# The head of a decoder layer's last stage: order of the second tile's scores, fill matmuls, and VectorE's order

## What is computed

```python
x = x + matmul(fake_quant(layernorm(x)), fake_quant(ctx))      # "x_product"
h = layernorm(x)
q = h @ Wq_w.T                    # router, 16 columns
scores = q @ keys.T               # 64 experts
gate = softmax over the 16 largest of each row, 0 elsewhere
z = (h @ A_w.T)                   # 512 columns, 8 for each expert, times gate
x = x + z_gated @ B_w.T * 2       # "out_product"
```

## Time and profile before

| | |
|---|---|
| time, median of 3 runs | 1102.18 us (1101.66 to 1102.24) |
| the profiled execution | 1102.29 us |
| its span | 1100.5 us |
| TensorE busy | 1064.6 us, 97% of the span |
| VectorE busy | 905.9 us, 82% |
| ScalarE busy | 530.8 us, 48% |
| mean granted clock of TensorE | 0.994 |

### The profile page before, as it was taken

One profiled execution on the slowest core, in us unless ns is written; L12 is line 12 of the kernel. 1 busy time (PEld: TensorE's weight loads), 2 busy tenths in 40 slices (PEclk: granted clock), 3 DMA queues, 4 the chain that ended last, 5 costly groups with the idle time before them and its releaser, 6 DMA issues.

```text
span 1100.5 us, 19648 instructions
## 1 busy us (share of the span) xinstructions
PE 1064.6 (97%) x6229; PEld 568.3 (52%) x6236; DVE 905.9 (82%) x1861; ACT 530.8 (48%) x1081; POOL 407.9 (37%) x423
## 2 busy tenths in 40 slices
PE   6999989999999999999999999999999999969998
PEld 5976544555555555555555555555555554434443
DVE  7979588988797878788888888787978799888973
ACT  5665465555444545454545455454445454233420
POOL 2239555544343435344342444353434233000000
PEclk9999999999999999999999999999999999989999
DMA  8026156654454455454544554554445389224442
GB/s 318 11 96 237 52 101 149 147 141 96 126 136 114 99 138 138 107 131 114 136 101 118 133 119 113 132 124 114 107 118 138 81 195 248 90 44 84 104 97 86
DMA packets 229601, 135.74 MB, mean 123 GB/s; under 512 B 200112, under 2 KB 202288, under 8 KB 228656
## 3 DMA queue, kind: packets, MB, share of 16 engines
q1 hardware_dynamic: 229552, 135.11, 48.5%
HBM read 68.23 MB, written 17.83 MB: 78 GB/s over the span
## 4 chain that ended last, share of the span: by engine, by line
PE 86%; DVE 8%; ACT 2%; issue 2%; DMA 1%; POOL 1%; POOLq 0%; DVEq 0%; ACTq 0%; SPq 0%
PE ps L1712 82%; PE ps L1965 2%; ACT prob L1042 1%; DVE prob L1435 1%; DVE wo_sb L1196 1%; DVE h_b L1196 1%; PE ps L2036 1%; PE ps L1726 1%; DMA wq_sb<-wo_in 1%; DVE x_sb L1417 1%; DVE prob_t L1196 1%; DVE o_t L1196 0%; DVE wq_sb L1196 0%; DVE prob_s L1196 0%; DMA prob_t<-prob_s 0%
## 5 line engine op out<-in xcount | busy, mean ns | idle before, releaser
L767 POOL TENSOR_SCALAR prob<-prob,row_inv 128x128 f32<-128x128 f32 (+3 forms) x256 | 198.9, 796 | 442.3 <-DVE row_inv L1406 442.3
L1712 PE MATMUL ps<-wo_sb,o_t 128*128 128x512 f16 x1536 | 351.7, 379 | 1.8 <-DVE x_sb L1417 1.7
L1712 PE MATMUL ps<-h_b,wq_sb 128*128 128x512 f16 x1524 | 346.3, 382 | 0.0
L1042 ACT ACTIVATE prob<-prob,neg_max 128x128 f32<-128x128 f32 (+3 forms) x256 | 140.6, 550 | 223.8 <-DVE neg_max L1441 223.8
L1712 PEld LDWEIGHTS ps<-h_b,wq_sb 128*128 128x128 f16 x1524 | 148.8, 99 | 179.1 <-issue 5.9
L1712 PEld LDWEIGHTS ps<-wo_sb,o_t 128*128 128x128 f16 x1536 | 147.1, 98 | 170.5 <-DVE x_sb L1417 5.8
L1417 DVE SCALAR_TENSOR_TENSOR x_sb<-ps,x_sb 128x512 f32<-128x512 f32 x256 | 174.4, 686 | 51.4 <-PE ps L1712 50.4
L1712 PE MATMUL ps<-prob_t,v_sb 128*128 128x128 f16 (+2 forms) x960 | 115.9, 273 | 7.0 <-DMA prob_t<-prob_s 7.0
L1712 PE MATMUL ps<-k_t,q_t 128*128 128x512 f16 (+3 forms) x768 | 114.8, 299 | 0.2
L1435 DVE CUSTOM_DVE_ANT_0 prob<-ps,mask 128x512 f32<-128x512 f32 (+3 forms) x256 | 110.3, 484 | 2.3 <-issue 1.6
L1712 PEld LDWEIGHTS ps<-prob_t,v_sb 128*128 128x128 f16 x960 | 83.2, 98 | 36.9 <-DMA prob_t<-prob_s 7.9
(11 more groups left out here) (147 smaller groups left out, 1140.8 us busy)
## 6 DMA issues: line engine op xcount, KB each, us to landing
wq_in<-in_wq SPq DMA_DIRECT2D x64, 256.0 KB, 3.5
wo_in<-in_wo SPq DMA_DIRECT2D x32, 512.0 KB, 3.9
side_in<-in_ctx SPq DMA_DIRECT2D x16, 512.0 KB, 4.3
kv_parts<-wo_sb SPq DMA_DIRECT2D x7, 1024.0 KB, 5.4
x_sb<-in_x SPq DMA_DIRECT2D x8, 512.0 KB, 9.4
ctx_quantised<-side_out SPq DMA_DIRECT2D x16, 256.0 KB, 2.9
h_b<-ctx_quantised SPq DMA_DIRECT2D x2, 2048.0 KB, 10.6
out<-x_sb SPq DMA_DIRECT2D x8, 512.0 KB, 2.9
```

What stands on the lines that cost most here:

```text
L767: ins = nc.gpsimd.tensor_scalar(at, at, row_inv[:, u % 2, q:q + 1], S_P, ALU.mult, ALU.mult)
L1042: ins = nc.scalar.activation(at, at, ACT.Exp, bias=neg_max[:, n % 2, q:q + 1], scale=SOFTMAX, accum_out=row_sum[:, n % 2, q:q + 1])
L1712: ins = nc.tensor.matmul(out_, lhs(i), rhs(j), start=start and n == 0, stop=stop and n == 3 * len(pairs) - 1)
```

## The change

All of it is in the head of the last stage; the matmul, vector and activation work of the tiles stays as it is, but for the following.

- TensorE: six constant matmuls (`fill`) ahead of turn_h3(0) and seven behind it. They read constants and write PSUM bank 0, which nobody reads then. scores(1) comes directly behind scores(0), ahead of x_product(2). Tile 1's h3 is transposed by TensorE in the midst of scores(0), behind 5 of its 8 z tiles. The keys product comes behind 2 z tiles, not 4, in every tile. Behind that: x_product(2), out_product(0, *), x_product(3), out_product(1, *), scores(2), and from i = 4 the loop as before.
- SyncE: no DMA transposes for h3 of tile 1; the head's order is written out, with store(0) ahead of turn_h3(3) and store(1) ahead of turn_gated(2).
- ScalarE and VectorE: tile 1's parts of h3 are split from PSUM; the orders of both are written out up to i = 3. VectorE's gate code is moved into `gate_z(t)` unchanged. The semaphore counts follow (`h3_splits`, `h3_dmas`).

```diff
@@ h3_dmas @@
-    return 32 * ((t + t % 2) // 2)
+    return 32 * (t // 2)
+
+
+def h3_splits(t):
+
+    return 2 * t + 2 if t < 2 else t + 3
...
+TURN_FILL, ROUTER_FILL = 6, 7
...
@@ SyncE @@
             def turn_h3(t):
-                sp.wait_ge(h3_hi, t + 2)
-                sp.wait_ge(x_done, 2)
-                if t >= 2:
-                    sp.wait_ge(z_done, t - 1)
+                sp.wait_ge(h3_hi, h3_splits(t))
+                sp.wait_ge(z_done, t - 1)
                 sp.dma_start_transpose(blocks(h3_t[:, t % 2, 0, :]), h3_s[:, t % 2, 0, :]).then_inc(h3_landed[t % 2], 16)
...
             turn_rounded(2)
-            for i in range(1, TT + STEPS_AHEAD):
+            turn_gated(0)
+            turn_rounded(3)
+            turn_gated(1)
+            turn_h3(2)
+            turn_rounded(4)
+            store(0)
+            turn_h3(3)
+            store(1)
+            turn_gated(2)
+            turn_rounded(5)
+            for i in range(4, TT + STEPS_AHEAD):
                 if i < TT:
                     turn_h3(i)
                 if i - 1 < TT - 1:
                     turn_gated(i - 1)
                 if i + STEPS_AHEAD < TT:
                     turn_rounded(i + STEPS_AHEAD)
-                if i >= 2:
-                    t = i - 2
-                    sp.wait_ge(out_done, 2 * t + 2)
-                    sp.dma_start(out[t], x_sb[:, t, :]).then_inc(stored, 16)
+                store(i - 2)
...
@@ ScalarE @@
             def h3_high(t):
-                if t == 0:
+                if t < 2:
                     for j in range(2):
-                        act.wait_ge(h3_turned, j + 1)
-                        split_hi(h3_t[:, 0, 0, j * HALF:(j + 1) * HALF], ps[:, H_BANK[j], :], h3_hi, S_H)
+                        act.wait_ge(h3_turned, 2 * t + j + 1)
+                        split_hi(h3_t[:, t, 0, j * HALF:(j + 1) * HALF], ps[:, H_BANK[j], :], h3_hi, S_H)
...
-            h3_apply(0)
-            h3_high(0)
-            scale_rows(STEPS_AHEAD)
-            for i in range(1, TT + 1):
-                if i > 1:
-                    copy_small(i - 1)
-                if i < TT:
-                    h3_apply(i)
-                if i == 1:
-                    copy_small(0)
-                    sum_rows(STEPS_AHEAD)
-                t = i - 1
...
+            h3_apply(0)
+            h3_high(0)
+            copy_small(0)
+            h3_apply(1)
+            h3_high(1)
+            scale_rows(2)
+            weigh(0)
+            copy_small(1)
+            sum_rows(2)
+            z_high(0)
+            scale_rows(3)
+            weigh(1)
+            z_high(1)
+            sum_rows(3)
+            h3_apply(2)
+            h3_high(2)
+            scale_rows(4)
+            sum_rows(4)
+            copy_small(2)
+            h3_apply(3)
+            h3_high(3)
+            weigh(2)
+            scale_rows(5)
+            z_high(2)
+            for i in range(4, TT + 1):
+                copy_small(i - 1)
+                if i == 4:
+                    sum_rows(5)
+                if i < TT:
+                    h3_apply(i)
+                weigh(i - 1)
                 if i < TT:
                     h3_high(i)
                 if i + STEPS_AHEAD < TT:
                     scale_rows(i + STEPS_AHEAD)
-                z_high(t)
+                z_high(i - 1)
...
@@ VectorE @@
             turn2 = quantise_start(2)
+            bias3(1, turn3)
             quantise_apply(2, turn2)
-            bias3(1, turn3)
+            turn2 = quantise_start(3)
+            h3_split(1)
             quantise_end(2)
-            for i in range(1, TT + STEPS_AHEAD):
-                if 1 < i < TT:
+            gate_z(0)
+            quantise_apply(3, turn2)
+            fold(2)
+            z_split(0)
+            quantise_end(3)
+            gate_z(1)
+            x_half(2, 0)
+            z_split(1)
+            turn3 = x_end(2)
+            turn2 = quantise_start(4)
+            bias3(2, turn3)
+            quantise_apply(4, turn2)
+            out_add(0, 0)
+            fold(3)
+            h3_split(2)
+            out_add(0, 1)
+            quantise_end(4)
+
+            x_half(3, 0)
+            turn3 = x_end(3)
+            turn2 = quantise_start(5)
+            bias3(3, turn3)
+            quantise_apply(5, turn2)
+            out_add(1, 0)
+            h3_split(3)
+            fold(4)
+            out_add(1, 1)
+            gate_z(2)
+            z_split(2)
+            quantise_end(5)
+
+            for i in range(4, TT + STEPS_AHEAD):
...
@@ TensorE @@
+            def fill(count):
+
+                pe.wait_ge(x_qt_copied, 2)
+                for _ in range(count):
+                    nc.tensor.matmul(ps[:, TURN_BANK, :], ones[:, :], ctx_sum[:, 0, 0:HALF], start=True, stop=True)
...
-            def turn_h3():
-
-                pe.wait_ge(h3_done, 1)
+            def turn_h3(t):
+
+                pe.wait_ge(h3_done, t + 1)
                 for j in range(2):
+                    if t == 1:
+                        pe.wait_ge(h3_lo, j + 1)
...
             def scores(t):
                 if t == 0:
-                    pe.wait_ge(h3_lo, 2)
                     pe.wait_ge(router_lo, 1)
                     pe.wait_ge(wq_lo, 7 * (CYCLES - 1) + 11 + KT // 2)
+                if t < 2:
+                    pe.wait_ge(h3_lo, 2 * t + 2)
+                else:
+                    pe.wait_ge(h3_landed[t % 2], h3_dmas(t))
                 if t >= 1:
-                    pe.wait_ge(h3_landed[t % 2], h3_dmas(t))
                     pe.wait_ge(s_copied, t)
 
                 for n in range(2 * KT):
...
-                z_part(t, range(0, KT // 2))
+                z_part(t, range(0, 2))
                 pe.wait_ge(r_copied, t + 1)
                 nc.tensor.matmul(ps[:, SMALL_BANK, S_COL:S_COL + EXPERTS], r_q[:, t % 2, :], keys_sb[:, :],
                                  start=True, stop=True).then_inc(s_done, 1)
-                z_part(t, range(KT // 2, KT)).then_inc(z_done, 1)
-
-            turn_h3()
+                z_part(t, range(2, 5))
+                if t == 0:
+                    turn_h3(1)
+                z_part(t, range(5, KT)).then_inc(z_done, 1)
+
+            fill(TURN_FILL)
+            turn_h3(0)
+            fill(ROUTER_FILL)
             scores(0)
-            for i in range(2, TT + STEPS_AHEAD):
+            scores(1)
+            x_product(2)
+            out_product(0, 0)
+            out_product(0, 1)
+            x_product(3)
+            out_product(1, 0)
+            out_product(1, 1)
+            scores(2)
+            for i in range(4, TT + STEPS_AHEAD):
```

More of the change, by code:

```diff
@@ L642, in turn_gated, with store @@
                 sp.dma_start_transpose(blocks(z_t[:, t % 2, 1, :]), z_s[:, t % 2, 1, :]).then_inc(z_landed[t % 2], 16)
+            def store(t):
+                sp.wait_ge(out_done, 2 * t + 2)
+                sp.dma_start(out[t], x_sb[:, t, :]).then_inc(stored, 16)
             turn_rounded(2)
-            for i in range(1, TT + STEPS_AHEAD):
+            turn_gated(0)
[9 more added lines that the diff above has]
+            for i in range(4, TT + STEPS_AHEAD):
                 if i < TT:
@@ L1161, in z_high, with weigh @@
                 split_hi(z_s[:, t % 2, 0, :], gated, zt_hi, 1.0)
[L1163 to L1174 removed]
+            def weigh(t):
                 act.wait_ge(best_done, t + 1)
@@ L1642, in z_split, with gate_z @@
                     split_lo(z_s[:, t % 2, 1, :], gated, z_s[:, t % 2, 0, :], zt_lo, 1.0)
+            def gate_z(t):
+                dve.wait_ge(s_copied, t + 1)
+                link(nc.vector.max(best[:, t % 2, 0, :], score[:, t % 2, :]))
+                nc.vector.tensor_scalar(neg_best[:, t % 2:t % 2 + 1], best[:, t % 2, 0, 0:1], -1.0, None, ALU.mult)\
+                    .then_inc(best_done, 1)
+                link(nc.vector.match_replace(left[:, t % 2, 0, :], best[:, t % 2, 0, :], score[:, t % 2, :], TAKEN))
+                link(nc.vector.max(best[:, t % 2, 1, :], left[:, t % 2, 0, :]))
+                link(nc.vector.match_replace(left[:, t % 2, 1, :], best[:, t % 2, 1, :], left[:, t % 2, 0, :], TAKEN))
+                dve.wait_ge(weighted, t + 1)
+                link(nc.vector.scalar_tensor_tensor(gate[:, t % 2, :], left[:, t % 2, 1, :], TAKEN, weight[:, t % 2, :],
+                                                    ALU.is_equal, ALU.mult, accum_out=gate_sum[:, t:t + 1]))
+                dve.wait_ge(z_done, t + 1)
+                if t >= 1:
+                    dve.wait_ge(zt_hi, t)
+                    dve.wait_ge(zt_lo, t)
+                nc.vector.scalar_tensor_tensor(
+                    gated.rearrange("p (e r) -> p e r", r=RANK),
+                    ps[:, z_bank(t), :].rearrange("p (e r) -> p e r", r=RANK), Z_OUT,
+                    gate[:, t % 2, :].unsqueeze(2).to_broadcast([P, EXPERTS, RANK]), ALU.mult, ALU.mult)\
+                    .then_inc(z_gated, 1)
+                link(nc.vector.reciprocal(gate_inv[:, t:t + 1], gate_sum[:, t:t + 1]))
```

(9 more changed lines are left out.)

27 lines of the change are left out of this document (14 added, 13 removed).

## The result

The changed kernel takes 1095.9 us (median of 5, 1095.14 to 1097.14), the kernel before, run beside it, 1102.18 us; the ratio is 0.9948, 95% interval 0.9935 to 0.9961. 1095.4 was forecast.

What follows compares the result with a forecast made beforehand. TensorE was taken as the bound, only its idle or low-clock time winnable: 9.4 us won in the head, less stalls 0.2, 1.0 and 1.6, 6.8 by the sum; 1102.2 - 6.8 = 1095.4 us, range 1092.6 to 1099.

Steps and rivals of the forecast that it cites:

- The sum: Last stage's head to scores(4): each engine's operations added in the new order; scores(4) at 1029.15, not 1035.93, 6.8 us won.
- VectorE's backlog: Behind the head: VectorE's step 14.71 us against TensorE's 15.39, catching up only 0.7 a step; stalls 0.2, 1.0 and 1.6.
- Rival A: VectorE's delay doesn't reach TensorE; gain up to the whole 9.4 us, 1092.8; chance 0.10.
- Rival B: Fills don't hold the clock at scores(0); VectorE's chain 0.9 us later, 1096.3, up to 1097.5; chance 0.12.
- what the fills are for: Thirteen constant matmuls around tile 0's transposes: clock stays up, router product 1.00 us and z at full speed.
- The clock as a fixed price: Router product and twelve matmuls of scores(1), behind 3.5 us without a matmul: one clock drop costs 2.93 us.
- Rival D: New short TensorE stalls each drop the clock, 2.93 us each; all four 1104.5, two about 1099.5; chance 0.08.
- no stall: Keys product of scores(1), behind 2 z tiles: ScalarE's copy done at 979.25, so no stall, cover 0.05 us.
- SyncE's order: store(0) and store(1) ahead of turn_h3(3) and turn_gated(2) hold nothing up; extra transpose time taken as 0 us.

Runs made afterwards that it cites:

- the short folds: Changed kernel with fold adding only 8 of 1024 columns for tiles 2 to 7, for timing alone: 1094.18 us, stage 122.12.
- The orders up to tile 4: Changed kernel, VectorE and ScalarE doing what leads to h3 first for tiles 3 and 4: 1096.35 us; also with the copy ahead of sum_rows(6): 1095.8 us.
- the order up to tile 5: Kernel with h3 work first for tiles 3 and 4 and the copy ahead of sum_rows(6), same turn added for tile 5: 1094.56 us.
- bias3(1) late: Changed kernel with bias3(1) behind quantise_apply(2) again: 1099.31 us, stage 127.00; with 8 constant matmuls in the wait: 1098.3 us, stage 125.83.
- the four with h3 first: Changed kernel reordered for h3 at tiles 3 and 4 (1096.35 us); cumulatively copy ahead of sum_rows(6) (1095.8), tile 5 too (1094.56), stores behind transposes (1094.36).

## Why the prediction was right, and where not

**The sum.** The head's start at 987.0 for out_product(0, 0) was 987.08; scores(2), (3), (4) and (5), predicted at 1001.1, 1012.2, 1029.15 and 1044.5, came at 1001.09, 1012.08, 1029.09 and 1044.48. The stalls ahead of scores(3) and (4) were 0.72 and 1.56, where the sum had 1.0 and 1.6. It held because durations start to start, overlap included, were added in each engine's order, and each wait was compared with the other engine's sum. Adding busy time alone would have given VectorE 14.15 us a step, not 14.71, and too small a backlog.

**VectorE's backlog** (forecast 9.4 us won in the head, 2.8 given back): shown by the two stalls and by the short folds. Rival A, no backlog, fell. The orders up to tile 4 then only moved the wait to the next tile; the order up to tile 5 took it away, since what was put off fell into steps with room.

**Rival B**, that the fills don't do what they are for: in the changed kernel the clock stood at 1.00, and without the fills it stayed up too, so the 0.9 us at which I priced it were not tested. The step that failed is what the fills are for: they won 0.1 us, since I was wrong in taking the low clock of the earlier trace rows at 970 as what always follows that idle time.

**The clock as a fixed price.** This is the weakest part of the sum. I took one trace of the kernel before as the kernel. Of its 44 executions beside the experiments 4 have a mean clock of 0.997 and a median of 1099.1 us, 35 have 0.994 and 1102.0, one has 0.995 (1101.3), 4 have 0.991 or 0.992 and 1101.8 to 1103.9. The first two groups are 2.9 us apart, the price of the fall behind the long wait. That it is this fall that is missing in the first group is inferred from the size; no such execution has a trace, and the mean clock alone doesn't tell: the traces also have one or two falls at 146 to 182 us, far ahead of the stage, and it is these that make 0.998 (one) or 0.996 (two) of the changed kernel's mean. If it is so, the change wins 3.9 us against the first group and 6.8 against the usual one. That the forecast met the median, within 0.5 us, is in part luck: the one profiled execution was a usual one.

**Rival D**, that short waits drop the clock: not in the changed kernel (1.00 through its waits of 0.16 to 1.56 us; it falls only from 1092 us on, behind the last matmul, where it costs nothing), but the mechanism is real one size up: behind 2.25 us, with bias3(1) late, it fell in the trace and the times split into 1097.0 to 1097.6 and 1099.3 to 1099.8. The kernel before passed 2.41 us at full clock, so the length of the wait alone doesn't decide. The Trainium skill, page "TensorE: Matmul & The Clock Gate", section "A second HAM failure mode: psum-queue depth-cycling", tells of a clock that goes down and up where TensorE often idles for a short time between groups of matmuls. No run here shows that: the changed kernel, with five such waits, stays at 1.00, and the fall with bias3(1) late stands behind one longer wait.

**Two parts not priced by themselves.** The keys product behind 2 tiles, which I gave only "no stall", carries 1.1 us, by ScalarE's list behind the copy of the scores. bias3(1) ahead of quantise_apply(2) carries 1.8, and with the clock 3.0. The prediction's sum had the 1.8 (972.65 instead of 974.45, read from the row of before); the 1.04 of the experiment's expectation left out the wait of 0.66 for GpSimd. Both parts are inside the 6.83, since the sum was made from the whole new order.

**SyncE's order**: held as said; store(0) and store(1) delayed nothing in the changed kernel.

## What to carry to other kernels

When a wait is taken out of the bounding engine's list, add up every other engine's new list start to start until it has caught up: the gain is what the head wins less what the slowest of them then lacks, and if its load is close to the bound's (14.7 of 15.4 us here) that takes many steps. Putting off work on a nearly full engine pays only if it is put off into steps that have room; one step short and the wait comes back unchanged. Before a clock's fall is booked as a gain, look at many executions' mean clock. And look for what stands behind a producer in its engine's list as well as for who waits for it.

## What the runs showed of the hardware

About the same idle times of TensorE around tile 0's transposes ended at a granted clock of 0.50 in two traces (1.35 and 1.58 us in the kernel before; 1.36 and 1.58 in it with the long wait filled) and stayed at 1.00 in another (1.45 and 1.66, no fills), and 2.41 us passed at 1.00 where 2.25 did not. With constant matmuls in the wait the clock stayed at 1.00 (15 in that of 3.63 us, 8 in that of 2.25; one trace each). Two DMA transposes of h3, issued 1.28 us apart, were ready 3.2 us behind the second issue in the changed kernel and 4.0 to 4.2 in the four with h3 first.
